# Layer 0 of a spectral convolution: a full-array matmul split into array tiles, a small half-mean moved between engines, and a new order of the tile matmuls

## What is computed

```
# layer 0: rfft2 -> complex 3x3 convolution in the frequency domain (16 -> 16 channels) -> irfft2
x = x + irfft2( conv3x3_complex( rfft2( groupnorm(x) ) ) + bias )
# layer 1: a mean filter of 15 x 15
x = x + mean_filter_15x15( groupnorm(x) )
```

## Time and profile before

| what | value |
|---|---|
| median of 3 runs (lowest to highest) | 4111.79 us (4107.49 to 4116.27) |
| the profiled execution, its own time | 4116.43 us |
| its span, first to last instruction | 4114.6 us |
| mean granted TensorE clock | 0.957 of full speed |
| instructions | 122879 |
| PE / DVE / ACT / POOL busy | 90% / 77% / 64% / 64% of the span |

### The profile page before, as it was taken

The page is one execution under the profiler, slowest core; times in us unless marked ns, Lnnn a source line. Parts: engine busy times, 40 slices in busy tenths (PEclk is TensorE's granted clock), DMA queues, the critical chain, the costliest instruction groups (busy, mean ns, idle before and its releaser), DMA issues.

```text
span 4114.6 us, 122879 instructions
## 1 busy us (share of the span) xinstructions
PE 3688.1 (90%) x41056; PEld 2642.1 (64%) x41056; DVE 3153.9 (77%) x5926; ACT 2618.7 (64%) x4792; POOL 2634.6 (64%) x2177
## 2 busy tenths in 40 slices
PE   3299998998989989899898998899988998989988
PEld 1166676666766667566675666666676666766667
DVE  7778877787867878678786887778877787777876
ACT  0089833997249962599527993289833997349962
POOL 5078852887538865488546885378852887538865
PEclk8599999999999999899999999999999999999999
DMA  7411165111741128211381114711165111741114
GB/s 164 160 43 51 40 186 157 50 51 36 226 124 49 51 58 241 84 51 51 94 240 49 51 51 133 208 41 51 43 179 164 50 51 32 223 128 52 51 48 137
DMA packets 228435, 406.74 MB, mean 99 GB/s; under 512 B 98160, under 2 KB 173520, under 8 KB 215888
## 3 DMA queue, kind: packets, MB, share of 16 engines
q1 hardware_dynamic: 205776, 285.88, 24.2%
q10 hardware_dynamic: 22400, 117.46, 10.5%
HBM read 256.31 MB, written 146.80 MB: 98 GB/s over the span
## 4 chain that ended last, share of the span: by engine, by line
PE 70%; DVE 10%; POOL 9%; issue 6%; ACT 2%; DMA 1%; ACTq 1%; SPq 1%; DVEq 0%; POOLq 0%
PE p L554 21%; PE h_ps L622 14%; PE h_ps L445 13%; PE p L648 6%; PE p L483 4%; PE xt_ps L435 4%; POOL ob_all L1252 3%; POOL arena L1245 2%; PE h_ps L554 2%; PE p L598 2%; POOL ob_all L1254 2%; DVE ob_all L1177 2%; POOL arena L1268 2%; ACT arena L697 1%; DMA img<-in_x 1%
## 5 line engine op out<-in xcount | busy, mean ns | idle before, releaser
L554 PE MATMUL p<-arena,bd_all 64*64 64x512 f16 x16896 | 1220.2, 380 | 17.2 <-DVE ob_all L1109 8.8
L1245 POOL TENSOR_TENSOR arena<-arena 128x512 f16<-128x512 f32 x512 | 593.7, 1159 | 607.1 <-ACT arena L727 580.5
L554 PEld LDWEIGHTS p<-arena,bd_all 64*64 64x64 f16 x16896 | 613.8, 105 | 383.7 <-issue 188.5
L697 ACT ACTIVATE arena<-h_ps 128x512 f16<-128x512 f32 x512 | 305.7, 597 | 835.1 <-PE h_ps L622 594.7
L1303 POOL TENSOR_TENSOR arena<-img 128x512 f32<-128x512 f32 x392 | 498.7, 1273 | 467.4 <-PE h_ps L622 438.6
L445 PE MATMUL h_ps<-hilbert,arena 128*128 128x256 f16 x6144 | 763.4, 275 | 25.5 <-DVE arena L1082 16.6
L1254 POOL TENSOR_TENSOR ob_all<-ob_all,img 128x512 f32<-128x512 f32 x512 | 662.5, 1294 | 82.9 <-POOL ob_all L1252 72.9
L445 PEld LDWEIGHTS h_ps<-hilbert,arena 128*128 128x128 f16 x6144 | 603.1, 98 | 148.4 <-issue 18.7
L1252 POOL TENSOR_TENSOR ob_all<-ob_all 128x512 f32<-128x512 f32 x512 | 653.7, 1277 | 26.4 <-DVE ob_all L1115 26.4
L1082 DVE SCALAR_TENSOR_TENSOR arena<-h_ps,arena 128x512 f16<-128x512 f32 x512 | 354.1, 692 | 390.3 <-ACT arena L741 389.4
L733 ACT ACTIVATE arena<-xt_ps 128x1024 f16<-128x1024 f16 x512 | 517.4, 1011 | 37.3 <-PE xt_ps L435 37.3
(11 more groups left out here) (164 smaller groups left out, 4537.4 us busy)
## 6 DMA issues: line engine op xcount, KB each, us to landing
out<-ob_all SPq DMA_DIRECT2D x512, 256.0 KB, 4.4
bd_all<-bd_dram SPq DMA_DIRECT2D x512, 192.0 KB, 2.3
img<-in_x ACTq DMA_DIRECT2D x168, 512.0 KB, 7.1
img<-in_x ACTq DMA_DIRECT2D x112, 256.0 KB, 4.9
wrap_mat<-tab_wrap_h SPq DMA_DIRECT2D x512, 32.0 KB, 2.0
img<-in_x SPq DMA_DIRECT2D x24, 512.0 KB, 24.5
bd_dram<-ob_all SPq DMA_DIRECT2D x16, 768.0 KB, 3.5
img<-in_x SPq DMA_DIRECT2D x16, 256.0 KB, 6.8
```

The costliest lines, as they stand in the source:

```text
L554: m = mm(bank[out_half * HP:(out_half + 1) * HP, :], low(half, 6 * lm + (j if own else j + 1)), (g_part if own else h_part)(half, lp), sta ...
L1245: G.tensor_tensor(gp[s][:, 1, :], g32, gp[s][:, 0, :], ALU.subtract).then_inc(g_split, 1)
```

## The change

1. The wrap matmul of 128 x 128 becomes four of 64 x 64. Two (the lower half of its input partitions) come in round 3 of the lower pairs, two (the upper half) in round 9 of the upper pairs. So both sides now have ten rounds from round 0 on: lower p0, wrap, p1, p2; upper p1, p2, p0, wrap. Of each bank the side that opens it changes with that.
2. In rounds 4 and 7, where the lower pair waits for a bank, the upper pair is issued ahead of it; in the other rounds lower comes first.
3. The wait for `x1_done` goes to the start of the mix, that for `t2_done` from round 1 to round 3, that for `v_wrap` (row 0 only) from the end of the mix to round 3.
4. The half-means are made by DVE in one instruction on 128 x 2 (`half_mean`, for row n-3 in slot n, between `wave_terms` and `low_hilbert`, with a wait for `x1_whole` of row n-7), no longer by ACT in two. ACT's `add_half_row` and POOL's `presum` run one slot later (four and five slots behind), so that one more of each stands behind the last row.

```diff
+                    if first > 0:
+                        pe.wait_ge(x1_done, PRIMED + n - (NG - 1))
                     pe.sem_inc(mix_step, 1)
-                    first_half = [(p1[:], 2)] * 3 + [(p0[s], 0)] * 3 + [(p2[:], 4)] * 3
...
+                    def wrap_terms(half, closes):
+                        for out_half in (half, 1 - half):
+                            m = mm(p0[s][out_half * HP:(out_half + 1) * HP, :],
+                                   wrap_mat[s][half * HP:(half + 1) * HP, out_half * HP:(out_half + 1) * HP],
+                                   wrap_row[half * HP:(half + 1) * HP, :], start=False, stop=closes,
+                                   skip_group_check=True)
+                        return m
+                    def lower(r):
+                        if r < 3:
+                            half_terms(p0[s], 0, r, 0, True, False)
+                        elif r == 3:
+                            if first == 0 and s == 0:
+                                pe.wait_ge(v_wrap, b + 1)
...
+                            wrap_terms(0, False).then_inc(p0_half, 1)
+                        elif r < 7:
                             if r == 4:
                                 pe.wait_ge(p1_half, n + 1)
...
+                            m = half_terms(p1[:], 2, r - 4, 0, False, True)
...
+                        else:
                             if r == 7:
+                                pe.wait_ge(p2_half, n + 1)
...
+                            m = half_terms(p2[:], 4, r - 7, 0, False, True)
...
+                    def upper(r):
+                        if r < 3:
+                            m = half_terms(p1[:], 2, r, 1, True, False)
...
+                        elif r < 6:
+                            if r == 3:
+                                pe.wait_ge(t2_done, PRIMED + n)
...
+                            m = half_terms(p2[:], 4, r - 3, 1, True, False)
...
+                        elif r < 9:
+                            if r == 6:
                                 pe.wait_ge(p0_half, n + 1)
...
+                            half_terms(p0[s], 0, r - 6, 1, False, False)
+                        else:
+                            wrap_terms(1, True).then_inc(p0_ready, 1)
...
+                    for r in range(10):
+                        for part in ((upper, lower) if r in (4, 7) else (lower, upper)):
+                            part(r)
...
-                    act.wait_ge(x1_counted, n + 1)
-                    for a in range(2):
-                        ins = nc.scalar.activation(half_row[:, s, a:a + 1], stat[:, t, 1 + 3 * a:2 + 3 * a], ACT.Identity,
-                                                   bias=known[:, t, a:a + 1], scale=-0.5)
-                    ins.then_inc(half_made, 1)
...
+                    if t >= 4:
+                        add_half_row(n - 4, i * NG + s - 4, s)
...
+                def half_mean(n, t, s, first):
...
+                    if first * NG + s >= NG:
+                        dve.wait_ge(x1_whole, n - NG + 1)
+                    dve.wait_ge(x1_counted, n + 1)
+                    V.scalar_tensor_tensor(half_row[:, s, :], stat[:, t, 1:6:3], -0.5, known[:, t, :],
+                                           ALU.mult, ALU.add).then_inc(half_made, 1)
...
+                    if t >= 3:
+                        half_mean(n - 3, i * NG + s - 3, (s - 3) % NG, first - (s < 3))
...
-                    slot(t // NG, t % NG, t // NG, sum_t=t - 4 if t >= 4 else None)
...
+                    slot(t // NG, t % NG, t // NG, sum_t=t - 5 if 5 <= t <= R + 5 else None)
```

More of the change, by code:

```diff
@@ L561, in mix @@
                     pe.wait_ge(t1_done, PRIMED + n)
+                    if first > 0:
+                        pe.wait_ge(x1_done, PRIMED + n - (NG - 1))
                     pe.sem_inc(mix_step, 1)
-                    first_half = [(p1[:], 2)] * 3 + [(p0[s], 0)] * 3 + [(p2[:], 4)] * 3
[L564 to L574, removed]
-                                pe.sem_inc(mix_step, 1)
[L576 to L584, removed]
+                    def wrap_terms(half, closes):
[11 more added lines that the diff above has]
+                                pe.wait_ge(v_wrap, b + 1)
+                                pe.sem_inc(mix_step, 1)
+                            wrap_terms(0, False).then_inc(p0_half, 1)
+                        elif r < 7:
                             if r == 4:
@@ L587, in mix @@
                                 pe.sem_inc(mix_step, 1)
+                            m = half_terms(p1[:], 2, r - 4, 0, False, True)
+                            if r == 6:
+                                m.then_inc(p1_ready, 1)
+                        else:
                             if r == 7:
+                                pe.wait_ge(p2_half, n + 1)
+                                pe.sem_inc(mix_step, 1)
+                            m = half_terms(p2[:], 4, r - 7, 0, False, True)
+                            if r == 9:
+                                m.then_inc(p2_ready, 1)
+                    def upper(r):
+                        if r < 3:
+                            m = half_terms(p1[:], 2, r, 1, True, False)
+                            if r == 2:
+                                m.then_inc(p1_half, 1)
+                        elif r < 6:
+                            if r == 3:
+                                pe.wait_ge(t2_done, PRIMED + n)
+                                pe.sem_inc(mix_step, 1)
+                            m = half_terms(p2[:], 4, r - 3, 1, True, False)
+                            if r == 5:
+                                m.then_inc(p2_half, 1)
+                        elif r < 9:
+                            if r == 6:
                                 pe.wait_ge(p0_half, n + 1)
                                 pe.sem_inc(mix_step, 1)
[L591 to L598, removed]
+                            half_terms(p0[s], 0, r - 6, 1, False, False)
[4 more added lines that the diff above has]
+                            part(r)
                 front(0, 0, 0)
@@ L795, in slot @@
                         nc.scalar.activation(wrap_high[:], p0[2], ACT.Identity, scale=sc[:, 27:28]).then_inc(v_high, 1)
-                    if t >= 3:
-                        add_half_row(n - 3, i * NG + s - 3, (s + 1) % NG)
+                    if t >= 4:
+                        add_half_row(n - 4, i * NG + s - 4, s)
                 for s in range(NG):
@@ L805, in image @@
                     slot(T // NG - 1, s, T // NG - 1)
-                for t in range(T - 3, T):
+                for t in range(T - 4, T):
                     add_half_row(b * T + t, t, t % NG)
@@ L1148, in layer0 @@
                 wave_terms(b * T + T - 1, T - 1, (T - 1) % NG, T // NG)
+                half_mean(b * T + T - 3, T - 3, (T - 3) % NG, T // NG - 1)
                 for t in (T - 2, T - 1):
                     finish_row(b * T + t, t, t % NG, T // NG)
+                for t in (T - 2, T - 1):
+                    half_mean(b * T + t, t, t % NG, T // NG - 1)
                 dve.wait_ge(half_made, (b + 1) * T)
@@ L1284, in layer0 @@
                     split_g(b * T + t, t)
-                for t in range(R + 5):
-                    slot(t // NG, t % NG, t // NG, sum_t=t - 4 if t >= 4 else None)
-                assert (R + 5) % NG == 0
-                with pool.Fori((R + 5) // NG, T // NG - 1) as i:
+                for t in range(R + 9):
+                    slot(t // NG, t % NG, t // NG, sum_t=t - 5 if 5 <= t <= R + 5 else None)
+                assert (R + 9) % NG == 0
+                with pool.Fori((R + 9) // NG, T // NG - 1) as i:
                     for s in range(NG):
@@ L1291, in layer0 @@
                 for t in range(T - NG, T):
-                    slot(t // NG, t % NG, t // NG, sum_t=t - 4 if t - 4 >= T - R else None)
+                    slot(t // NG, t % NG, t // NG, sum_t=t - 5 if t - 5 >= T - R else None)
                 add_terms(b * T + T - 1, T - 1, (T - 1) % NG, T // NG)
-                for t in range(T - 4, T):
+                for t in range(T - 5, T):
                     presum(b * T + t, t)
```

## The result

The changed kernel takes **4086.83 us** (median of 4 runs, 4080.91 to 4087.45) against 4110.07 before (4 runs): ratio 0.9938, 95% interval [0.9921, 0.9955]. That is 23 us faster, a third of the 71 that were forecast; the measured time lies above the stated range of 4010 to 4070. The profiled execution has a span of 4084.5 us, 30.1 less than before.

The account below looks back on a forecast made before the run. TensorE was taken to bound layer 0's rows; 1.4 + 47 rows x 0.16 = 8.9 us an image, 71 for eight, takes 4116.4 to 4045, and the runs' median lying 4.6 lower gives 4041 us; range 4010 to 4070.

Parts of the forecast that it names:

- The bound: Layer 0 rows: TensorE, busy for all 4.48 us of a row's period, sets the time, with ACT close at 4.30.
- ACT's relief alone: Half-means off ACT: 0.46 us and a gap less a row, counting nothing by itself because ACT was not the bound.
- The 4.46 taken for ACT's work: ACT's old row, L754 to L754 without idle: at 4.32 it would have taken back nearly all of the saving.
- the forecast 4.32: Layer 0's row period after the change: mixes 4.32 us apart, from 4.48, by 0.16 less a row.
- Lower's round 7 takes p2 from it at 1.18 + 0.53 = 1.71: Mix, second handoff: lower gets p2 0.53 us after upper's round 5 starts, also 1.71 on its own beat.
- The rule that I weighed: TensorE: the skill says matmuls start and end strictly in program order; by it the change would give half of the sum.
- one common order: Rival, mix: lower's round 5 holds upper's round 5, saving only 0.05 to 0.08 a row; 4076 us, chance 0.08.
- The end of the layer: Last rows of layer 0: two DVE half-means of 0.22 replace L1152's 0.55 wait for ACT, costing zero.
- The second gap: Sign of being wrong: a gap in lower at round 7, besides the forecast 0.17 ahead of round 4.
- Steady rows of the half-mean: DVE's new instruction between t2 and `low_hilbert`: zero, covered by idle time; up to 0.22 a row if uncovered.
- POOL's sums: Rows 5 to 15, bound by POOL: rows 2 to 15 give about 1.4 us together, not 2.1.
- First row: `v_wrap` wait in mid-mix: cover 0.7 us, else 1.5; half-clock Hilbert up to 1.3 us either way, counted as nothing.

Follow-up runs that it names:

- experiment 3: The kernel before with the changed kernel's new mix, half-means left on ACT: 4067.74 us, ratio 0.9894.
- experiment 4: The changed kernel with the old mix put back, so only the half-means' move to DVE remains: 4124.12 us, ratio 1.0042 to the kernel before.
- experiment 7: The kernel before with the new mix, upper issued first in rounds 4, 5 and 7, half-means left on ACT: 4039.65 us, ratio 0.9831.
- Experiment 1: The changed kernel with the upper pair issued first in round 5 too (rounds 4, 5, 7): 4028.20 us, ratio 0.9799.
- experiment 2: The changed kernel with lower issued first in every round: 4088.06 us, ratio 0.9947.
- experiment 5: The changed kernel, with POOL waiting after the first of its last five sums until DVE has corrected the means: 4076.50 us, ratio 0.9918.
- experiment 8: Changed kernel with upper first in rounds 4, 5, 7 and POOL's wait for stat_fixed (4016.41 us), DVE's half-mean moved behind L1139: 4029.79 us.

## Why the prediction was wrong

**The bound: right.** TensorE sets the rows before and after; ACT's relief alone brings nothing (experiments 3, 4), and it does keep ACT from becoming the bound, though at 4.28 and not yet at 4.42. The 4.46 taken for ACT's work was 4.34 to 4.36 when it really bound (experiment 7); at the forecast 4.32 ACT would by that have taken back 0.02 to 0.04 a row (an estimate), not "nearly all".

**The step that failed: "Lower's round 7 takes p2 from it at 1.18 + 0.53 = 1.71".** I applied one handoff price to both handoffs. The 0.53 was read where everything issued ahead of the giver's last pair had ended before that pair did. The first one kept it (from 331.59 to lower's round 4 at 332.13: 0.54). The second one took 0.68, since upper's round 5 is told complete only after lower's round 5, which was issued ahead of it and starts 0.11 later. Experiment 1 shows it by turning the two round and by the times of the semaphores, experiment 2 by letting upper's round 5 come later without loss. The rest of that working held, and one term was better than forecast: upper starts less than 0.01 behind lower, not 0.07. Without the failed step rows would be 4.28 apart, as in experiment 1; my 4.32 forecast a little less than that.

**The rule that I weighed.** I read from the earlier trace rows that upper's pair may start ahead of one issued before it, and put the whole rule aside (the Trainium skill, TensorE: Matmul & The Clock Gate, Part 3: matmuls start and end strictly in program order). The trace contradicts its half on starts. Of its half on ends the row says nothing, since the ends of matmuls are modelled in a profile, but the semaphores bear it out. The trace before held it already: upper's third pair on p2 starts at 333.96, yet its `p2_half` rises only at 334.52, 0.41 after the pair of lower's that was issued before it and started at 334.10. Nothing waited on it there. The rival "one common order" had the place and nearly the size (0.05 to 0.08 a row, measured 0.06) and was given 0.08.

**The end of the layer: wrong.** "Now two DVE instructions of 0.22 stand there: zero". The price came from a row where POOL was idle; here POOL's sums run beside them. Together with L1180 it cost 1.4 us an image, 11 in all (experiments 4, 5). The second gap cost more: rows 15 to 62 gave 2.9 us an image where 7.5 was forecast, 37 us in all. L1152's 0.69 for 128 elements, against 0.22 for one, was already the sign: alone it takes 0.33. The Trainium skill has the rule (SBUF — State Buffer, Who interferes with whom): a DVE instruction with two SBUF inputs and a GpSimd instruction that reads SBUF exclude each other for a whole instruction. The trace agrees: 0.15 alone, 0.71 under L1282, and in experiment 8 all 481 half-means that began more than 0.15 us ahead of the end of a POOL instruction ended after it.

**Steady rows of the half-mean: right, partly by luck.** It took 0.15 in DVE's idle time, because POOL was idle too.

**POOL's sums:** still the bound of some four rows; 0.8 saved, not 1.4, mostly because each free row gave 0.06 and not 0.16.

**First row: cover right, clock not counted.** The wait in the middle of the mix cost nothing, since the Hilbert still waited for DVE (0.42). The half-clock dip vanished in all eight images (granted 0.50 before, 1.00 after), worth nearly all of the 1.67 us an image: the one image of the old mix without the dip (experiment 4) took 1.61 less than its neighbours. I had put it at nothing, with 1.3 either way. Why it vanished is open. TensorE's idle time now comes in two pieces (1.84 and 0.42 us, for 2.08 in one), and none of the 64 images of the eight kernels with the new mix had the dip; but of the 16 with the old mix one had none either, after 2.08 us in one piece.

**Open.** The start of layer 1 takes 7.1 to 8.9 us from the scale to its first box matmul, and which it is changes from kernel to kernel and image to image (7.9 before and 8.2 after in the first image, so 0.3 of the last 0.5 us of the table). From the scale to the next image it is 187.5 to 195.4 us over all traces, longer where TensorE spent more of it at half the clock (before: 195.4 us with 26.6 of them, 188.5 with 12.8). Over seven such stretches that is several us of a kernel's time. I did not follow it, so differences of that size between two kernels, such as 8 of the 19 us in experiment 3, are not explained.

## What to carry to other kernels

When one side of the array hands a bank to the other, count from the completion of everything that was issued ahead of the giver's last matmul: issue the giver first, and keep the other side's matmuls behind it. A tiny DVE instruction with two SBUF operands is priced by what POOL does at that moment, not by its size; look at POOL's timeline at each of its places, the last row included. Work taken off an engine that is not the bound pays only once another edit has made it the bound: time the parts together and apart.

## What the runs showed of the hardware

- Matmuls on different halves of the array's rows may start out of the order of issue (before: 333.96 for the seventh pair issued, 334.10 for the sixth), yet a later-issued one signals only after the earlier-issued one. From the start of a matmul to its signal it takes 0.40 us, and 0.54 where an earlier-issued one starts 0.14 later; the handoff is 0.68 us in that case, 0.54 otherwise (0.53 before).
- `scalar_tensor_tensor` on 128 x 2 with both tensors in SBUF: 0.15 us with POOL idle, 0.71 with 0.69 us of a POOL instruction left, up to 1.2 at the end of the layer; L996 on 128 x 1 went from 0.22 to 1.14 in the same way, L1180 on 128 x 128 from 0.33 to 1.42.
- TensorE's granted clock stayed at its upper level (2.4 GHz) from 221 to 227 us in the changed kernel after idle stretches of 1.84 and 0.42 us; before, an idle stretch of 2.08 us was followed by the lower one (1.2 GHz) from 221 to 224 us. In the second image of experiment 4 the upper level was kept after the same 2.08 us.
